# A decoder layer on one core: VectorE's work regrouped in cross-attention, and an earlier release of the experts' input tiles

## The reference

```
x = x + self_attention(layernorm(x))          # 8 heads of 64: blocks, selection and window, gated
x = x + cross_attention(layernorm(x), ctx)    # 16 heads of 8; keys are ctx (64) then x (256), causal
x = x + experts(layernorm(x))                 # 8 experts of 128 -> 512 -> 128, the two best per token
```

## Time and profile before

| | us |
|---|---|
| median of 3 runs | 1373.62 (1372.87 to 1380.2) |
| profiled execution, in all | 1380.81 |
| its span, first to last instruction | 1379.1 |
| mean granted clock of TensorE, as a share of full speed | 0.894 |

### The profile page before, as it was taken

How to read it: one execution, slowest core, us unless ns; L and a number is a source line. 1 busy time by engine, 2 the same in 40 slices (tenths; PEclk the granted TensorE clock), 3 DMA queues, 4 the chain that set the end, 5 groups by cost and what they waited for, 6 DMA issues and landing times.

```text
span 1379.1 us, 37192 instructions
## 1 busy us (share of the span) xinstructions
PE 1132.5 (82%) x13562; PEld 789.0 (57%) x13651; DVE 941.3 (68%) x3517; ACT 576.4 (42%) x1305; POOL 322.9 (23%) x422
## 2 busy tenths in 40 slices
PE   2599898989898999799588888788888878299992
PEld 1366666666666666566355555555555545188882
DVE  4578777877787878678466777776777777333334
ACT  1244343434443434244145444444554444055551
POOL 6212111111111111112100030311303031445452
PEclk9999999999998999899688989988898998599996
DMA  4000000000000002996000000000000000122225
GB/s 108 1 2 10 2 9 3 9 3 9 2 9 2 10 2 64 217 205 99 5 2 2 2 17 0 15 6 10 15 0 15 0 15 4 39 59 73 61 73 185
DMA packets 61204, 47.04 MB, mean 34 GB/s; under 512 B 6317, under 2 KB 55376, under 8 KB 60576
## 3 DMA queue, kind: packets, MB, share of 16 engines
q1 hardware_dynamic: 56496, 36.71, 12.5%
q0 software_dynamic: 4592, 8.60, 2.0%
HBM read 17.57 MB, written 28.64 MB: 34 GB/s over the span
## 4 chain that ended last, share of the span: by engine, by line
PE 63%; DVE 19%; issue 8%; DMA 4%; ACT 3%; POOL 2%; SPq 1%; DVEq 0%; POOLq 0%; ACTq 0%
PE ps L1656 6%; PE ps L1579 5%; DVE x_mneg L778 4%; PE ps L768 4%; PE ps L686 3%; PE ps L1632 3%; PE ps L1634 3%; PE ps L380 3%; DMA f_xs<-sorted_rows 3%; PE ps L849 3%; PE ps L1785 3%; PE ps L1668 3%; PE ps L1637 2%; PE ps L818 2%; PE ps L1424 2%
## 5 line engine op out<-in xcount | busy, mean ns | idle before, releaser
L838 ACT ACTIVATE x_E<-ps 128x512 f32<-128x512 f32 x256 | 153.2, 609 | 71.8 <-PE ps L818 69.6
L777 DVE TENSOR_REDUCE x_mneg<-ps 128x1 f32<-128x192 f32 x262 | 92.4, 353 | 102.0 <-PE ps L762 100.1
L768 PE MATMUL ps<-x_QM,x_KT 32*128 32x256 f16 (+2 forms) x771 | 108.0, 250 | 27.5 <-DVE x_QM L803 14.5
L778 DVE TENSOR_REDUCE x_mneg<-ps 128x1 f32<-128x320 f32 x262 | 125.7, 480 | 0.0
L1555 POOL TENSOR_TENSOR a_rope<-a_qraw,rope_sb 128x144 f32<-128x144 f32 x36 | 18.0, 499 | 414.5 <-ACT a_sq L1511 414.5
L768 PE MATMUL ps<-x_KT,x_QT 24*128 24x192 f16 (+1 forms) x524 | 110.6, 294 | 0.8 <-issue 0.8
L1675 ACT COPY a_OT<-ps 128x448 f32<-128x448 f32 x65 | 34.6, 532 | 180.0 <-PE ps L1656 180.0
L1645 ACT ACTIVATE a_E<-ps 128x512 f32<-128x512 f32 x128 | 77.3, 604 | 73.0 <-PE ps L1637 72.9
L478 POOL DMA_INDIRECT expert_rows<-f_ost,f_idu x78 | 76.7, 983 | 80.2 <-DVE f_ost L447 64.5
L768 PEld LDWEIGHTS ps<-x_QM,x_KT 32*128 32x128 f16 x771 | 54.6, 96 | 68.6 <-issue 31.3
L1656 PE MATMUL ps<-a_E,a_V 128*64 128x64 f32 (+2 forms) x1300 | 85.8, 288 | 0.0
(11 more groups left out here) (363 smaller groups left out, 2898.1 us busy)
## 6 DMA issues: line engine op xcount, KB each, us to landing
sorted_rows<-pad_row SPq DMA_DIRECT2D x8, 2080.0 KB, 27.5
f_xs<-sorted_rows SPq DMA_DIRECT2D x39, 130.0 KB, 2.2
f_y<-expert_rows SPq DMA_DIRECT2D x4, 1024.0 KB, 7.1
ffn_raw<-in_L_ffn_W_dram SPq DMA_DIRECT2D x8, 256.0 KB, 2.6
out_dram<-f_y SPq DMA_DIRECT2D x8, 256.0 KB, 5.4
expert_rows<-f_ost,f_idu POOLq DMA_INDIRECT x78, 2.2
sorted_rows<-r_rows,r_posu POOLq DMA_INDIRECT x64, 2.3
ctx_all<-in_ctx_dram SPq DMA_DIRECT2D x1, 512.0 KB, 6.3
```

The costliest lines, as they stand in the source:

```text
L768: pe.matmul(out, weights, moving, start=start, stop=False, skip_group_check=True)
L777: dve.tensor_reduce(m[:, 0:1], S[:, 0:192], AX.X, ALU.max, negate=True)
L778: dve.tensor_reduce(m[:, 1:2], S[:, 192:512], AX.X, ALU.max, negate=True)\
L838: act.activation(self.E32[:, u % 2, h % 4, :], self.t_bank(h), ACT.Exp).then_inc(self.exp_done.sem, 1)
```

## The change

In cross-attention, VectorE's statistics (j = 11) and inputs (j = 13) of batch b+2 move from steps 11 and 13 to step 0. The router's two halves of the statistics move between them, one half in each batch. Both halves of `normalise` move to step 1 of the odd batch. POOL takes the root of batch 2i+3 ahead of the router's root. TensorE's and ScalarE's orders stay.

In the experts, the row numbers and the gates of a tile are copied out of `xs` in `dve_low`, into tiles with eight buffers, and the load into a buffer of `xs` waits for the low half of the tile four before.

```
-        self.idu = f("idu", [self.OBUF, 2], U32)
+        self.idu, self.gate = f("idu", [2 * self.OBUF, 2], U32), f("gate", [2 * self.OBUF, 2])
...
     def dve_low(self, dve, t):
+        g, xs = t % (2 * self.OBUF), self.xs[:, t % self.XBUF, :, :]
         dve.wait_ge(self.xhi_ready, t + 1)
+        dve.tensor_copy(self.idu[:, g, :], xs[:, :, 0])
+        dve.tensor_copy(self.gate[:, g, :], xs[:, :, 1])
...
     def dve_rows(self, dve, st, t, e):
-        b, xs = t % self.OBUF, self.xs[:, t % self.XBUF, :, :]
+        b, gate = t % self.OBUF, self.gate[:, t % (2 * self.OBUF), :]
-        dve.tensor_copy(self.idu[:, b, :], xs[:, :, 0])
...
-            last = dve.tensor_scalar(self.ost[:, b, s, :], o32[:, s, :], xs[:, s, 1:2], None, ALU.mult)
+            last = dve.tensor_scalar(self.ost[:, b, s, :], o32[:, s, :], gate[:, s:s + 1], None, ALU.mult)
...
     def sync(self, sp):
-                sp.wait_ge(self.XT_ps, t - self.XBUF + 1)
-                sp.wait_ge(self.o_ready, t - self.XBUF + 1)
+                sp.wait_ge(self.xlo_ready, t - self.XBUF + 1)
...
     def dve_round(self, dve, sts, i, routed):
-                self.dve_early(dve, st, b + 2, h)
-                if routed and par == 0:
+                if h == 0:
+                    self.dve_early(dve, st, b + 2, 11)
+                    if routed:
+                        r.stats_of(dve, i - 1, par)
+                    self.dve_early(dve, st, b + 2, 13)
+                if h == 15:
+                    self.dve_early(dve, st, b + 2, 15)
+                if routed and par == 1:
                     if h == 1:
-                        r.stats_of(dve, i - 1, 0)
-                    if h == 12:
-                        r.stats_of(dve, i - 1, 1)
-                    if h == 14:
                         r.normalise(dve, i - 1, 0)
-                if routed and par == 1:
-                    if h == 0:
                         r.normalise(dve, i - 1, 1)
...
     def gpsimd(self, pool):
             rstd(i * 2 + 2)
+            rstd(i * 2 + 3)
             r.pool_rstd(pool, i - 1)
             r.pool_gates(pool, i - 1)
-            rstd(i * 2 + 3)
             r.pool_scatter(pool, i - 1)
```

More of the change, by code:

```diff
@@ L477, in gpsimd @@
             for s in range(2):
-                pool.indirect_dma_start(k.y_dram[:, :], bass.IndirectOffsetOnAxis(ap=self.idu[:, b, s:s + 1], axis=0),
+                pool.indirect_dma_start(k.y_dram[:, :], bass.IndirectOffsetOnAxis(ap=self.idu[:, t % (2 * self.OBUF), s:s + 1], axis=0),
                                         self.ost[:, b, s, :], None, bounds_check=2 * self.N - 1, oob_is_err=False)\
```

## The result

The changed kernel takes 1387.91 us in the median of 15 runs (1383.23 to 1407.37), the kernel before 1379.36 in 15 runs (1372.87 to 1383.37): 1.0067 times the time before, 95% interval 1.0047 to 1.0088. It is slower by 0.7%, where 0.7% faster was forecast. (The ratio leaves out the one slow run, of 1407.37 us.) The profiled executions stand 2.4 us apart in span (1379.1 and 1381.5); their stages show where both signs come from.

What follows compares the result with a forecast made beforehand. TensorE, busy 82% of the span, sets the pace, though in the cross stage it and VectorE wait for each other. Experts -13.9 and cross +4.1 us sum to -9.8: from 1373.6 to 1363.8 us, range 1352 to 1379.

Steps and rivals of the forecast that it cites:

- Experts: Expert stage: loads issued earlier leave TensorE's own 3.32 us as the tile step; -13.9 us, between -12 and -14.8.
- The bound of -14.8: Expert stage: the largest gain allowed, 14.8 us, if nothing is left over.
- The wait on POOL and the clock behind it: Even batches, rounds 2 to 7: VectorE waits about 5 us for POOL's root, net +1.7 us; lower TensorE clock, +1.6.
- Steps 11 to 14: Cross stage, even batches: VectorE work taken from these head steps gives -2.75 us per batch, between -2.0 and -3.3.
- Odd batches: Cross stage: router rows come late, delaying ScalarE's exponential and TensorE's step 3; +1.2 us, 2.1 at lower clock, 0.2 at higher.
- Sum: Cross stage: six rounds at +1.75 us give +10.5, batches outside them -6.4; with the experts -9.8 us in all.
- The first three batches: Cross stage: the unrouted round's two batches at about -1.9 us each, and round 1's even batch at -3.0.
- Cross: Whole cross-attention stage: a net loss of +4.1 us.
- the base: Time of the kernel before, taken as 1373.6 us, to which the forecast change of -9.8 us was added.
- Rival (c): Cross stage: the wait on POOL decides, a round costs 6.0 us; kernel slower by 16 us, time 1389; chance 0.10.
- (b): Cross stage: step-14 stall vanishes, clock stays up, wait on POOL shorter; about -8 us, time 1352; chance 0.22.
- (d): Expert stage: loads early but tile stays near 3.7 us behind another wait; -2 us, time 1376; chance 0.08.

## Why the prediction was wrong

**Experts: right.** -13.9 forecast, -15.1 by stage, -14.4 alone. The tile step is TensorE's own 3.32 us, and the two copies on VectorE stayed hidden. The bound of -14.8 was 0.3 short, within what profiles differ (160.1 to 161.5 us in the nine executions with this part).

**The wait on POOL and the clock behind it: right.** From the row positions to step 10 of the even batch 24.50 became 28.51, +4.0, where 2.56 of waiting and 1.6 of clock were put down. Before step 2 the even batch lost 2.78 us, behind it 1.49. The six waits on the root are 2.76 to 4.54 us, 3.8 in the mean, for about 5, and TensorE's stand at step 2, forecast as some 5 us, is 3.30 at 939.39 and 3.6 at most.

**Steps 11 to 14: right.** From step 10 to the next projection even batches went from 9.48 to 6.92, -2.55, for -2.75. The waits at step 14 of the even batches are 0.85, as forecast. The positions came 0.85 us earlier, for up to 0.95.

**Odd batches: wrong, and this is the step that failed.** I put +1.2 between 0.2 and 2.1; it is +3.6. The term priced ScalarE's lateness alone, and what is left with the clock held up, 0.7 to 1.4, is close to that. It left out that TensorE, standing 1.49 us for the shift and 1.60 behind ScalarE, loses its clock for the following steps: 2.2 us or more on top, outside the bound. I charged the fall of the clock to the new stand in even batches, and read the same kind of stand in odd ones as a shift of the chain. The reasoning that a projection at the upper clock would lower the cost to 0.2 did not hold: at 962.64 the values do run at the upper level, TensorE then arrives earlier at step 3, stands longer, and the clock falls there instead of at the boundary. The Trainium skill (TensorE: Matmul & The Clock Gate, "HAM oscillation — how this bites in real kernels") has, for waits on transfers, the price paid in each step that contains one. Here the waits are on other engines, and the odd batches' 0.50 from 969.30 to 976.10 agrees; I had applied that rule to one of the two new waits only.

**Sum.** A round costs +4.0 - 2.55 + 3.6 - 0.85 = +4.2 us rather than +1.75, six rounds +25.2 for +10.5. The first three batches gave back 8.0 where 6.8 were put; the other batches make up +2.6. Cross +19.8 for +4.1, and the experts' gain no longer covers it. Of the 24 us between 1363.8 and the median of 1387.91, 5.7 are the base: the kernel before takes 1379.36 in 15 runs, for the 1373.62 of three. Rival (c), at a chance of 0.10, gave 1389 and comes nearest, but by luck: it named the wait on POOL at its upper bounds, and POOL's terms came as forecast, while the odd batches went past even the 2.1 that it took for them. Rivals (b) and (d) fell: the clock is 0.83 over the cross stage, after 0.87 before, and the tile step is 3.32.

## What to carry to other kernels

A gap in which an engine is idle is cover for moved work only if what that work waits for is there by then: follow each of its waits into the queue of the engine that serves it, and look at what stands ahead there (eight scatters, a copy of rows). Price the granted clock behind every new stand of TensorE, on whichever engine's account it comes, not only behind the largest. When a move goes wrong, change the neighbours' order before undoing the move: here that turned +0.7% into -2.5%, of which the experts' part alone is -0.9%.

## What the runs showed of the hardware

POOL's eight scatters hold its queue for 10.6 us from the first step to the root behind them, 0.96 us each and 0.30 between; a root of 0.73 us asked for meanwhile comes when they are out. The lower clock can last long: 17.1 us with TensorE busy 15.5 of them, in two batches out of six whose code was the same. And useless products can be cheap: 168 of them in the whole kernel, 12 in a batch, came with a kernel some 11 us shorter, where they filled a stand; where they did not fill one, they took what they gave.
